# A three-stage transformer block on one core: panels, query quantisation, value halves and output weights re-ordered at the edges of the stages

## What is computed

```python
# cross attention, 16 heads of 64, one softmax over all 8192 context tokens
q = (layernorm(x) @ Wq + bq) / 8;  k, v = split(ctx @ Wkv + bkv)
q = fq_sym(q, per row and head);  k = fq_sym(k, per row and head);  v = fq_sym(v, per column, over all tokens)
p = fq_unsigned(softmax(q @ k.T), per row)
x = x + (p @ v) @ Wp + bp
# causal self attention with rotary embedding, per batch of 128 tokens
x = x + attention(layernorm(x), Wq2, Wk2, Wv2, Wo)
# feed forward of width 2816 with four-bit weights, silu(gate) * up, RMS norm of its result
x = x + rms(ffn(layernorm(x)))
# fq_sym: s = max|a| / 127, round(a / s) * s;  fq_unsigned: s = max / 255
```

## Time and profile before

| | us |
|---|---|
| median of 3 executions | 2761.11 (2759.78 to 2761.98) |
| profiled execution, whole | 2763.46 |
| its span, first to last instruction | 2761.6 |
| PE busy | 2529.8 (92%) |
| DVE busy | 2068.7 (75%) |
| ACT busy | 1142.1 (41%) |
| POOL busy | 859.8 (31%) |
| mean granted TensorE clock | 0.964 of full speed |

### The profile page before, as it was taken

How to read it: one execution, slowest core, us unless ns; L and a number is a source line. 1 busy time by engine, 2 the same in 40 slices (tenths; PEclk the granted TensorE clock), 3 DMA queues, 4 the chain that set the end, 5 groups by cost and what they waited for, 6 DMA issues and landing times. The chain is left out here.

```text
span 2761.6 us, 42893 instructions
## 1 busy us (share of the span) xinstructions
PE 2529.8 (92%) x16296; PEld 1286.5 (47%) x16296; DVE 2068.7 (75%) x2971; ACT 1142.1 (41%) x1096; POOL 859.8 (31%) x381
## 2 busy tenths in 40 slices
PE   6999999999999999999778888888868999999998
PEld 3444444444444444444344545545444458444443
DVE  7788778777877778777689999999965434766664
ACT  3322222222222222222489999999982124311100
POOL 0232222322232222321455646556521460111100
PEclk9999999999999999999799999999988995899999
DMA  6134433444344433444568888888863222000000
GB/s 252 48 89 122 122 99 94 119 122 106 93 112 122 122 97 94 120 122 103 149 169 195 202 211 187 196 210 189 201 176 117 102 74 55 1 16 16 1 4 31
DMA packets 557343, 321.54 MB, mean 116 GB/s; under 512 B 401968, under 2 KB 533296, under 8 KB 552368
## 3 DMA queue, kind: packets, MB, share of 16 engines
q1 hardware_dynamic: 557232, 319.91, 45.0%
HBM read 149.95 MB, written 69.21 MB: 79 GB/s over the span
## 5 line engine op out<-in xcount | busy, mean ns | idle before, releaser
L1253 DVE TENSOR_SCALAR_CACHE_REDUCE at_sc<-at_score 128x1024 f32<-128x1024 f32 x512 | 601.6, 1219 | 22.5 <-PE at_score L1132 14.8
L1351 ACT ACTIVATE at_sc<-at_sc,at_bias,at_qs 128x4096 uint16<-128x4096 f32 x128 | 484.9, 3792 | 1.1 <-DVE at_bias L1265 1.1
L646 PE MATMUL kv_vacc<-kv_whi,kv_xthi 128*128 128x512 f16 x1024 | 388.8, 380 | 5.9 <-PEq L274 5.9
L646 PE MATMUL kv_vacc<-kv_wlo,kv_xthi 128*128 128x512 f16 x1024 | 388.7, 380 | 0.0
L646 PE MATMUL kv_vacc<-kv_whi,kv_xtlo 128*128 128x512 f16 x1024 | 388.6, 379 | 0.0
L654 PE MATMUL kv_kacc<-kv_wk,q_t 128*128 128x512 f16 x1536 | 348.7, 380 | 5.8 <-DVE kv_key L799 5.8
L725 ACT ACTIVATE q_t<-q_t 128x512 f16<-128x512 f32 x128 | 77.1, 626 | 505.7 <-POOL q_t L909 332.7
L907 POOL TENSOR_TENSOR q_t<-kv_rows 128x512 f32<-128x512 f32 x32 | 41.4, 1295 | 701.2 <-DMA kv_rows<-in_ctx 614.4
L654 PEld LDWEIGHTS kv_kacc<-kv_wk,q_t 128*128 128x128 f16 x1536 | 150.5, 98 | 188.6 <-issue 8.7
L731 ACT ACTIVATE o<-kv_key 128x1024 f16<-128x1024 f32 x64 | 67.7, 1057 | 397.7 <-DVE kv_key L818 397.7
L654 PE MATMUL kv_kacc<-kv_wk,kv_xthi 128*128 128x512 f16 x768 | 228.4, 379 | 0.7 <-DVE kv_xtlo L503 0.7
(11 more groups left out here) (230 smaller groups left out, 4243.5 us busy)
## 6 DMA issues: line engine op xcount, KB each, us to landing
kv_rows<-in_ctx SPq DMA_DIRECT2D x64, 512.0 KB, 6.9
values<-kv_val SPq DMA_DIRECT2D x32, 1024.0 KB, 6.4
keys_turned<-o SPq DMA_DIRECT2D x32, 1024.0 KB, 5.1
at_v_raw<-values SPq DMA_DIRECT2D x16, 2048.0 KB, 8.4
at_kt<-keys_turned SPq DMA_DIRECT2D x32, 512.0 KB, 5.2
x<-keys_turned SPq DMA_DIRECT2D x31, 512.0 KB, 5.1
x<-in_x SPq DMA_DIRECT2D x2, 2048.0 KB, 8.6
kv_wk<-in_wq SPq DMA_DIRECT2D x2, 2048.0 KB, 13.0
```

The source lines that it names most:

```text
L646: last = nc.tensor.matmul(v_acc[2 * s + c][:], a[s][:, k, :], b[:, c, k, :], start=(k == 0 and q == 0), stop=(k == KD - 1 and q == 2))
L1253: nc.vector.tensor_scalar(sc[n % 2][:, c * SC:(c + 1) * SC], score[pos % 2][:], 1.0, None, ALU.mult, ALU.max, accum_out=part_max[n % 2][:, ...
L1351: nc.scalar.activation(prob[n % 2][e], sc[n % 2][:, e * EC:(e + 1) * EC], ACT.Exp, bias=bias[n % 2][:], scale=qs_pair[j][:, t:t + 1], accu ...
```

## The change

Five things are re-ordered; no product is added or left out.

- Value panel 3 is split on DVE before any query sum is taken, and `kw.low` 2 and 3 too; the low parts of the first context rows move ahead of panel 2's.
- The queries are quantised in pieces: two maxima of 1024 columns in pairs 1 and 2, the small scale operations in pair 3, two multiplications in pairs 4 and 5, the rounding in pair 6, each right after the first `take_key` of its pair. The factor 1/8 goes into the scales, and the pass L398 falls away. ACT's two copies go from after pairs 3 and 4 to after pairs 7 and 8. In the last pair ACT makes the last high part of the keys before it copies queries 4 to 7.
- POOL quantises each head's values in two halves (six instructions), `v_quantised` counts halves, and PE waits for the second at the head's first `sums`.
- The first two chunks of scores go ahead of the maxima's transposes on PE, and the spreading goes behind chunk 3; DVE reduces the maxima after its second copy.
- The `Wp` stages are allocated for the whole program; key room 1, raw values, `key`, `val` and the value weights' high parts lie in them. Panel 0 is loaded in slot 6 of the last pair of heads (after the last values are quantised), panel 1 after the last scores, `x` in slot 5. `project("pp")` splits panel 0 before the turner.

```diff
@@ start_loads
-            for n in range(2):
-                panels.load(sp, n)
+            while panels.next_load < 2:
+                panels.load(sp, panels.next_load)
@@ project, vector
+            for m in split_first[:low_first]:
+                panels.low(dve, m)
             turner.vector(dve)
-            for m in split_first:
+            for m in split_first[low_first:]:
                 if ahead is not None and m == 2:
                     kw.sums(dve, 0)
+                    for s in range(2):
+                        tokens.low(dve, 0, s)
                 panels.low(dve, m)
             if ahead is not None:
                 kw.low(dve, 0)
                 kw.sums(dve, 1)
                 kw.low(dve, 1)
                 kw.sums(dve, 2)
-                for s in range(2):
-                    tokens.low(dve, 0, s)
+                kw.low(dve, 2)
+                kw.low(dve, 3)
...
-                if ahead is not None and n == 0:
-                    kw.low(dve, 2)
-                    kw.low(dve, 3)
@@ keys_and_values, scalar
+                key_high(i, first, 0, 2)
                 if last:
                     for n in range(4, 8):
                         queries_out(n)
-                key_high(i, first, 0, 2)
@@ keys_and_values, vector
+            body(1, False, False, first_maxima)
+            body(2, False, False, last_maxima)
+            body(3, False, False, lambda: queries.scales(dve))
+            body(4, False, False, first_rows)
+            body(5, False, False, last_rows)
+            body(6, False, False, lambda: queries.round(dve))
+            with dve.Fori(7, LAST_PAIR) as i:
@@ attend_quantised, sync
+                    if n == SLOTS - 3 and last:
+                        sp.wait_ge(filled, CH * T * (HEADS - 1))
+                        sp.dma_start(x[:], x_d).then_inc(chip.rows_loaded, 16)
+                    if n == SLOTS - 2 and last:
+                        sp.wait_ge(v_quantised, 2 * HEADS)
+                        panels.load(sp, 0)
...
+            sp.wait_ge(filled, CH * T * HEADS)
+            panels.load(sp, 1)
@@ attend_quantised, gpsimd
+                for half in range(2):
+                    tiles = slice(half * KVT // 2, (half + 1) * KVT // 2)
+                    nc.gpsimd.tensor_tensor(v_raw[:, tiles], v_raw[:, tiles],
+                                            vi_head[:].unsqueeze(1).to_broadcast((P, KVT // 2, HD)),
+                                            ALU.mult).then_inc(v_step, 1)
...
@@ attend_quantised, tensor: sums
+                if k == 0 and n % T == 0:
+                    pe.wait_ge(v_quantised, 2 * (g // T) + 2)
@@ dma_sums
-                        pe.wait_ge(v_quantised, head + 1)
+                        pe.wait_ge(v_quantised, 2 * head + 1)
@@ before slot 0, tensor
-            for k in range(KD):
-                last = nc.tensor.transpose(spread[1][:, k * P:(k + 1) * P], vmax[:, k * P:(k + 1) * P], ident32[:])
-            last.then_inc(vs_turned, 1)
             inputs_ready(0, 0)
             for c in range(CH + AHEAD):
                 scores(c // CH, c // CH, c % CH)
                 if c == 1:
+                    for k in range(KD):
+                        last = nc.tensor.transpose(spread[1][:, k * P:(k + 1) * P], vmax[:, k * P:(k + 1) * P],
+                                                   ident32[:])
+                    last.then_inc(vs_turned, 1)
+                if c == 3:
                     pe.wait_ge(vs_reduced, 1)
@@ build
-                project(chip, "pq", panels, 0, 2, (0, 1, 2), ((3,), ()),
+                project(chip, "pq", panels, 0, 2, (0, 1, 2, 3), ((), ()),
...
-                    stats=(stats, x))
+                    stats=(stats, x), high_first=1, low_first=1)
```

More of the change, by code:

```diff
@@ L261, in low, with project @@
                                             op1=ALU.subtract).then_inc(self.lo_ready, 1)
-def project(chip, tag, panels, first, count, split_first, split_after, rows, addend, out, added=None, beside=None, high_first=0,
+def project(chip, tag, panels, first, count, split_first, split_after, rows, addend, out, added=None, beside=None, high_first=0, low_first=0,
             stats=None, ahead=None):
@@ L770, in body @@
                         queries_out(n)
-                key_high(i, first, 0, 2)
-                if last:
                     value_abs(i, 1)
@@ L781, in _ @@
             body(0, True, False)
-            for i in range(1, 5):
+            for i in range(1, 9):
                 body(i, False, False)
-                if i > 2:
-                    queries.scalar(act, i - 3)
-            with act.Fori(5, LAST_PAIR) as i:
+                if i > 6:
+                    queries.scalar(act, i - 7)
+            with act.Fori(9, LAST_PAIR) as i:
                 body(i, False, False)
@@ L838, in value_max, with body @@
                 nc.vector.tensor_tensor(vmax, vabs, vmax, ALU.max).then_inc(v_ready, 1)
-            def body(i, first, last):
+            def body(i, first, last, quantised=None):
                 if not first:
@@ L958, in values, with attend_quantised @@
             .then_inc(self.v_loaded, 16)
-def attend_quantised(chip, q_t, exp_scale, heads, v_scale, col, twice, o, ident32, ident16, x_d, x, stores):
+def attend_quantised(chip, q_t, exp_scale, heads, v_scale, col, twice, o, ident32, ident16, x_d, x, stores, panels):
     nc = chip.nc
@@ L1997, in build @@
         start(chip, a["ident"], ident32, ident16, x_d, x, x_loaded)
+        wt_stage = [chip.sb(whole, f"wt_stage{j}", [P, KD, HALF], F32)[:] for j in range(2)]
+        flat = [stage.rearrange("p k n -> p (k n)") for stage in wt_stage]
+        panels2 = WeightPanels(chip, None, "wt", [h for w in ("wp", "wq2", "wk2", "wv2", "wo") for h in halves(a[w])],
+                               stage=wt_stage)
         with ExitStack() as cross:
@@ L2041, in build @@
             mask = chip.sb(c, "mask", [P, P], F32)
-            panels = WeightPanels(chip, c, "wt", [h for w in ("wp", "wq2", "wk2", "wv2", "wo") for h in halves(a[w])])
+            panels = panels2
+            panels.place(chip, c)
             WORDS_AT = 8 * D + NSC * HALF // 2
```

126 lines of the change are left out of this document (66 added, 60 removed).

## The result

The changed kernel takes 2726.4 us (median of 4 runs, 2723.9 to 2727.4), the kernel before 2761.5 (4 runs, 2759.8 to 2762.0): ratio 0.9871, 95% interval 0.9858 to 0.9884. It is 35.0 us faster; the forecast was 2728, between 2721 and 2739. The profiled execution took 2726.34 us with a span of 2724.6 us, 37.0 less than the 2761.6 before.

A forecast was written before the change was run, and what follows sets the result against it. PE's work plus its waits bound the kernel, with DVE and ACT full in the attention. Edge gains 6.1 + 7.2 + 2.5 + 6.8 + 7.0 + 3.1 = 32.7 us off 2763.5 profiled give 2730.8, median 2728.4; range 2721 to 2739.

The forecast's parts named there:

- Edge 1: Start of the key and value stage, value panel split first: 4.6 us sooner plus 1.6 of half clock, 6.1 together.
- Edge 2: Key and value stage, queries quantised in pieces: wait of 5.62 us and 1.6 of half clock go, 7.2 us.
- Edge 3: End of the last key and value pair, ACT's high part before query copies: 2.5 us, between 2 and 3.
- Scores in front: Opening of the attention, same DVE work reordered ahead of the first exponent: counted as nothing, between -1 and +1.
- Edge 4: Attention heads 0 and 1, values quantised by halves: 6.8 us for head 0 and 7.0 for head 1.
- a play of 1.4: Heads 0 and 1: slack of chunk 7's scores before DVE fetches them, 1.4 us, covering head 0's 0.6 to 0.9 wait.
- the 4.9 us of four copies: Heads 0 and 1: PE's new wait at the sums comes four chunks later, about four copies of 1.22 us.
- Edge 5: Way to the Wp matmuls, panel 0 loaded within the attention: 3.6 us sooner less 0.5 price, 3.1 us.
- The feared price in the attention: Loads of x and panel 0 beside the last turned probabilities: between 0 and 2 us, taken as 0.5.
- The rival of the port: At the Wp split, POOL's addition gets in front of DVE, which waits up to 8.7 us: median 2736.6, chance 0.25.
- One sign in the prediction: Steady stretch of the attention: a slot longer than 10.3 us would break the whole forecast.

The follow-up runs named there:

- edge 1 alone: The kernel before, with only value panel 3 and two key weights lowered before the query sums are taken: 2754.7 us, ratio 0.9972.
- the seven kernels of the table: The changed kernel and six variants of it, compared on when PE asks for head 0's second half of values; PE waits 2.36 to 3.24 us.
- edge 2 alone: The kernel before, with only the queries quantised in six pieces within pairs 1 to 6: 2752.3 us, ratio 0.9964.
- POOL early: The changed kernel, with POOL's addition of the bias to x waiting only for the row it reads: 2732.3 us, ratio 0.9893.
- two transfers: The changed kernel, with head 0's values loaded in two transfers, the first half as soon as the attention begins: 2722.7 us, ratio 0.9859.
- rows turned first: The changed kernel, with the turner before the split of panel 0, as in the kernel before: 2733.3 us, ratio 0.9902.
- Wp edge undone: The changed kernel, with x loaded after the last turned probabilities, Wp panels after the attention, turner first: 2731.7 us, ratio 0.9891.
- scores in front undone: The changed kernel, with the maxima of the values turned and reduced before the first scores again: 2726.9 us, ratio 0.9874.

## Why the prediction was right, and where it was not

**Edge 1.** The start came 4.36 us sooner (4.6 forecast), the pass, sums and takes as counted. The 1.6 us of clock come only because edge 2 removes the next stall too; edge 1 alone got 0.3 of them. (The prediction's own terms, 4.6 and 1.6, give 6.2 and not the 6.1 that it adds.)

**Edge 2.** With edge 1, 9.01 for both in the stage against 8.8. No piece of the query passes stopped PE.

**Edge 3.** 2.50 forecast and measured, and shown to be the order on ACT. Scores in front: nothing, as forecast.

**Edge 4.** The sum is right, 13.63 against 13.8, but partly by luck, and its split is not. Undone by themselves the halves are worth 11.9. From before to after 1.67 us of the 13.63 lie ahead of the first bias, where nothing was forecast, 3.5 in head 0 (37.4 to 33.9) and 8.4 in head 1 (19.12 to 10.68).

The step that failed is head 0, forecast at 6.8. The prediction let PE's second wait there be 0.6 us, inside a play of 1.4; it was 2.36 to 3.24 in the seven kernels of the table. POOL was ready 36.4 us after the barrier, as forecast (36.2), but PE asked at 33.6 (1360.21) and not at 35.6. The scores in front didn't move the request, since it comes at 34.18 without them. The request was worked out from one trace: there PE asked for the whole values 30.6 us after the barrier, and with edge 1 alone and edge 2 alone, where the attention is as before, it asked at 29.1 and 28.7; with the 4.9 us of four copies these give 34.0 and 33.6. Why it differs so between traces of the same code stays open. The wait was also followed by half clock in five of the seven, which I had allowed only for head 1.

Head 1 was taken at 7.0 with a wait of 2.8; undone by itself it is worth 7.0 with a wait of 1.33, which costs nothing (10.68 with no wait in POOL early). So this agreement is luck too. Where the wait was 2.75 (two transfers), it cost 2.85 (13.13 against 10.28), not the 2.0 that I took. There what head 0 was spared, head 1 paid; with the rows turned first head 0 was spared 1.4 and head 1 paid 0.25, so it isn't a rule.

**Edge 5.** 2.65 + 0.82 = 3.5 against 3.1. The first matmul came 12.2 us after the projection's first transposes could start, and not 11.3: behind the low part PE waited 0.75 us for the first bank and made sixteen more transposes in 3.46, where I had counted 3.2 for both. The feared price in the attention did not show: its last stretch is 19.11 us, and 17.9 to 19.9 over all kernels with and without these loads. One term was left out: the wait of 8.65 us before Wp was followed by half clock like those of the other edges, and the prediction put this at nothing. The 2.12 us by which the stretch of the Wp matmuls became shorter belong to that term: 0.8 of them stand between the changed kernel and the one with this edge undone, the rest is the kernel before, whose 47.83 is above all others.

**The rival of the port** had a chance of 0.25 and lost by 1.29 us, the distance between DVE's start and POOL's. The prediction said a margin of about 1 us. Its mechanism is shown. Its size depends on the lead: with POOL 3.5 us ahead DVE waits 5.2 us, and the kernel takes 2732.3 us, not 2737; the whole 8.6 us come where POOL leads by 0.2 or 0.4 us (a DVE pass of 13.05, at panel 1 in edge 1 alone and in Wp edge undone, where nobody waits for it).

**What no step named.** 1.88 us in the last stretch, where the code is the same. The way from ACT's table load to the end took 634.7 to 637.3 us over the kernels of this study. Two of them, by stretches of 300 us and the rest from that load (PE, PEld, DVE, ACT, POOL, clock, DMA share, GB/s), first the changed kernel, then the one with the scores in front undone:

```profile
2089.35:2389.35 300.00, 280.45 (x1322) 170.93 (x1323) 148.29 (x217) 93.27 (x196) 87.05 (x34) 0.84 0.19 54
2389.35:2724.60 335.25, 326.12 (x1511) 147.68 (x1509) 202.68 (x277) 32.12 (x55) 24.24 (x21) 0.99 0.04 14
```

```profile
2086.38:2386.38 300.00, 280.71 (x1312) 172.49 (x1313) 148.34 (x217) 93.73 (x196) 86.32 (x34) 0.83 0.20 54
2386.38:2723.70 337.32, 328.26 (x1521) 148.63 (x1519) 202.67 (x277) 32.12 (x55) 24.96 (x22) 0.99 0.04 14
```

DVE does the same work in both to 0.1 us, the granted clock is 0.84 against 0.83, and the second falls 2.1 us behind. The clock orders all fourteen traces: its mean over this way is 0.922 in the four that take 634.7 to 635.1 us, 0.919 in the three up to 635.4, 0.917 in the four from 636.0 to 636.4, and 0.915 in the three from 637.0 to 637.3. So about 2.6 us lie in how the clock falls in the short stages. The kernel before stood at 637.13, the slow end, and the changed one at 635.25; no edit is shown to decide it.

The forecast was 32.7 us, the profiled gain 37.0. The 4.3 between them are the 2.12 of clock at Wp, the 1.88 that no step named, and 0.3 over all the edges. The profiled execution of the kernel before was 2.0 above its median, so the medians differ by 35.0 only.

One sign in the prediction was badly set: a slot in the steady stretch longer than 10.3 us should have broken the whole. From the 9th to the 64th slot a slot takes 10.57 us on average in both kernels, so that sign was already there before.

## What to carry to other kernels

Price a removed stall with what follows it, everywhere: where PE comes back at half clock, the wait and the clock go together, but here the clock was saved in full only when the next stall went too. Splitting the work of a late producer helps until the last piece is what is waited for; from there only its start and its total count, so start it sooner, and check that the next round's start moves with it. Where two engines hold each other off, look at which of them starts first and by how much: here 1.3 us decided over 5. And before a difference of 1 or 2 us in one trace is explained, look at how much the same code differs there between kernels.

## What the runs showed of the hardware

The cost of returning from rest differs for one and the same stall: 5.62 us of waiting cost 1.5 us of half clock in the kernel before and 2.8 with edge 1 alone, and the pause at the start of the stage (5.91 and 6.10 us) cost 1.5 in the kernel before and 2.65 with edge 2 alone; a pause of 1.26 us cost none. In head 0 of the attention, waits of 2.36 to 3.24 us were followed by half clock in five of the seven kernels of the table, and waits of 2.74 and 3.10 us by full clock in the two others. The Trainium skill's page "TensorE: Matmul & The Clock Gate", in "Part 1: The HAM clock gate", says that the point where the fast clock sets in depends on when the first matmul comes, and gives ±500 ns for it. That it varies agrees. By the rows it came with the 9th matmul of the stage in the kernel before (82.33) and with the 14th with edge 2 alone (84.61), after first matmuls at 79.09 and 79.15; that is more than the page's ±500 ns, and the rows decide.

POOL's addition and DVE's pass over two tensors of SBUF, the on-chip memory, held each other off in all fourteen traces, in both orders, and the one held ended about its own time after the other: DVE passes 4.28 or 4.29 us after POOL (so they took 4.50 to 13.05 us instead of 4.42), additions 8.7 us after DVE (11.83 to 12.96 instead of 8.84). DVE's takes of turned rows, with one input in PSUM, were never held (0.68 to 0.69 us).

POOL's rate depends on the operand: 2048 columns take 4.52 us when one input is a row repeated over tiles (a multiplication) and 3.60 when it is one number per partition (an addition or subtraction). That it is the operand and not the operation, 4096 columns show: the addition of a repeated row to `x` takes 8.84 us, the addition of one number 7.01. Cutting them in two costs 0.34 us for a quarter of the values (6.26 against 5.92).
